# New instruction orders in the first unit and the last stage of a four-layer conditioned residual stack, with the last pair in halves and two pairs' x1 moved to ScalarE

## The reference, cut to what matters

```python
x = x + einsum('bct,bcd->bdt', x, w0[idx_a]) + bias0[idx_a][:, :, None]       # layer 0, mixes positions
h = silu(lora_linear(x, Wg, Ag, Bg, idx_a)) * lora_linear(x, Wu, Au, Bu, idx_a)
x = x + lora_linear(h, Wd, Ad, Bd, idx_a)                                     # layer 1, hidden size 2048
x = x + x @ W.T + (x @ A[idx_b].T) @ B[idx_b].T * scal[idx_b]                 # layer 2
x = x + einsum('bct,bcd->bdt', x, w3[idx_c])                                  # layer 3, mixes positions
# lora_linear(x, W, A, B, i) = x @ W + (x @ A[i]) @ B[i], rank 16, 8 adapters
```

## Time and profile before

| what | us |
| --- | --- |
| median of 3 runs | 735.73 |
| the runs | 731.42, 735.73, 737.94 |
| the profiled execution's own time | 731.5 |
| its span, first to last instruction | 729.7 |
| mean granted TensorE clock | 0.989 |
| TensorE matmul busy in the span | 697.1 |
| VectorE busy | 558.0 |
| POOL busy | 335.0 |
| ScalarE busy | 261.3 |

### The profile page before, as it was taken

The page is one execution under the profiler, slowest core; times in us unless marked ns, Lnnn a source line. Parts: engine busy times, 40 slices in busy tenths (PEclk is TensorE's granted clock), DMA queues, the critical chain, the costliest instruction groups (busy, mean ns, idle before and its releaser), DMA issues.

```text
span 729.7 us, 10894 instructions
## 1 busy us (share of the span) xinstructions
PE 697.1 (96%) x3658; PEld 596.3 (82%) x3658; DVE 558.0 (76%) x979; ACT 261.3 (36%) x470; POOL 335.0 (46%) x606
## 2 busy tenths in 40 slices
PE   8698999999999999999789999999999999989997
PEld 8576788888888888888668888888888888878996
DVE  8956968797978788789877878786969695865553
ACT  3433423232424232443333242332323231436554
POOL 5863544353435343438174544545353343235531
PEclk9899999999999999999999999999999999999999
DMA  8494843333333342504653232323432234213332
GB/s 245 116 173 134 248 135 102 115 102 116 104 120 109 118 124 85 102 22 159 218 130 106 80 106 84 104 84 100 133 103 84 61 92 162 69 51 102 121 116 94
DMA packets 91752, 84.39 MB, mean 116 GB/s; under 512 B 44721, under 2 KB 73393, under 8 KB 91697
## 3 DMA queue, kind: packets, MB, share of 16 engines
q1 hardware_dynamic: 79984, 52.73, 24.4%
q0 software_dynamic: 11392, 30.95, 14.5%
q10 hardware_dynamic: 320, 0.02, 0.0%
HBM read 70.57 MB, written 13.11 MB: 115 GB/s over the span
## 4 chain that ended last, share of the span: by engine, by line
PE 84%; DVE 10%; issue 4%; ACT 2%; POOL 0%; DVEq 0%; ACTq 0%
PE bank L1685 40%; PE bank L1810 21%; PE bank L1693 6%; PE bank L1820 4%; PE bank L1947 3%; PE bank L1953 3%; DVE XC L1158 2%; PE bank L1985 1%; PE bank L1926 1%; PE bank L1631 1%; PE bank L1655 1%; PE bank L1619 1%; DVE XA L1303 1%; DVE hid L1286 1%; DVE hs L1292 1%
## 5 line engine op out<-in xcount | busy, mean ns | idle before, releaser
L1685 PE MATMUL bank<-XC,WC 128*128 128x512 f32 x1344 | 336.1, 396 | 11.3 <-DVE XC L1158 5.2
L1685 PEld LDWEIGHTS bank<-XC,WC 128*128 128x128 f32 x1344 | 245.9, 190 | 60.1 <-issue 10.3
L1810 PE MATMUL bank<-hs,wds 128*128 128x512 f32 x768 | 185.9, 391 | 0.1
L1810 PEld LDWEIGHTS bank<-hs,wds 128*128 128x128 f32 x768 | 141.8, 188 | 28.5 <-DVE wds L1245 0.5
L545 POOL DMA_INDIRECT BL<-bgtab,poffs x96 | 99.4, 1035 | 132.3 <-PE bank L1693 90.0
L545 POOL DMA_INDIRECT BL<-butab,poffs x96 | 96.4, 1004 | 85.9 <-PE bank L1693 63.5
L815 ACT ACTIVATE hs<-hid 128x512 fp32r<-128x512 f32 x64 | 40.1, 630 | 173.4 <-DVE hid L1286 99.2
L1303 DVE TENSOR_TENSOR XA<-bank,XA 128x512 f32<-128x512 f32 x128 | 87.1, 685 | 19.0 <-PE bank L1810 13.1
L809 ACT ACTIVATE hid<-hid 128x512 f32<-128x512 f32 x48 | 30.3, 633 | 152.4 <-DVE hid L1269 79.7
L587 POOL COPY adsel<-ad_raw 128x32 f32 x256 | 43.5, 219 | 69.0 <-DVE ads L1250 64.7
L1693 PEld LDWEIGHTS bank<-UT,BL 128*128 128x128 f32 x384 | 61.7, 191 | 12.6 <-issue 4.4
(11 more groups left out here) (207 smaller groups left out, 855.8 us busy)
## 6 DMA issues: line engine op xcount, KB each, us to landing
RW<-in_L_cond_Wg_dram SPq DMA_DIRECT2D x16, 512.0 KB
RW<-in_L_cond_Wu_dram SPq DMA_DIRECT2D x16, 512.0 KB
RD<-in_L_cond_Wd_dram SPq DMA_DIRECT2D x16, 512.0 KB, 3.4
out_dram<-XB SPq DMA_DIRECT2D x16, 256.0 KB, 2.0
XB<-in_x_dram SPq DMA_DIRECT2D x8, 256.0 KB, 6.0
x1park<-XB SPq DMA_DIRECT2D x8, 256.0 KB
x2park<-XA SPq DMA_DIRECT2D x8, 256.0 KB
XA<-x1park SPq DMA_DIRECT2D x4, 512.0 KB, 7.1
```

Source lines behind the costliest of these rows:

```text
L1685: last = nc.tensor.matmul(psum[:, :], WC[:, t, left, a, k, :], XC[:, right, b, k, :], start=(first and k == 0 and n == 0), stop=(k == 1 an ...
L1810: last = nc.tensor.matmul(psD[j % 2][:, :], by_feature(wds[:, f, a, :])[:, j % KT, :], hs[:, f, b, j // KT * 512:(j // KT + 1) * 512], sta ...
```

## The change

- **Who makes x1.** `SUMMED = 6`: VectorE adds the biases for pairs 0 to 5 only; pairs 6 and 7 get them from TensorE's bias matmul and are copied by ScalarE. `s_xr` becomes two semaphores (one for each writer), asked through `x1_there`.
- **Start, TensorE.** 12 warming matmuls of 512 columns in place of 24 of 128, and none after the biases; pairs 8 and 9 go behind the first product P1, 10 and 11 behind P6, 14 and 15 ahead of the selects.
- **Start, VectorE and ScalarE.** New lists. T2 (and what it needs) comes ahead of B21, T3, B22, the B table and T1. The zeros of `w0second` and `w3bd` are written by ScalarE. `move_matrices` and `pass_rows` are earlier.
- **Start, POOL and SP.** `select_a` is split in two pairs of quads around pairs 12 and 13; `select_ad(0)` goes behind `gather_b(1, 1)`. The loads of A go ahead of B's and of four x pairs; the eight loads of the down adapters go behind `load_d(0)` and `load_b(1)`, both of which wait until TensorE has done pair 15.
- **Units 0 and 8.** The first silu is ahead of `raw_high`/`sums_high` (unit 0) or between them (unit 8). In unit 0 the sums u3 and half22 come ahead of U's weights on VectorE.
- **Last stage.** Down adapters' splits first on ScalarE, `ud_low(0)` ahead of `hs_low`, `lora_down(3)` behind `layer2(0)`, `ud_high(1)`/`ud_low(1)` earlier, `w3_low` later; pair 15 is done in two halves of 256 columns, and y of pair 14 is copied by VectorE.

```diff
-        XO = [[B11, B21, B22, T3, T2, T1, T4], [B11, B21, T3, T2, B22, T1, T4]]
+        XO = [[B11, T2, B21, T3, T1, B22, T4], [B11, B21, T3, T2, B22, T1, T4]]
...
+        SUMMED = 6
+        def x1_there(pairs):
+            return (s_xr[0], pairs) if pairs <= SUMMED else (s_xr[1], pairs - SUMMED)
...  (SP)
+                load_xin(HP)
+                load_xin(HP + 1)
+                load_a(0)
                 load_b(0)
-                for p in range(HP, HP + XIN):
+                for p in range(HP + 2, PAIRS - 2):
                     load_xin(p)
-                load_a(0)
                 store_b(0)
-                for p in range(HP + XIN, PAIRS):
+                for p in range(PAIRS - 2, PAIRS):
                     load_xin(p)
                 load_idx(2, idx_c)
                 load_u(0)
                 load_g(1)
-                sp.wait_ge(s_xr, HP)
+                load_d(0)
+                load_b(1)
+                sp.wait_ge(s_xr[0], SUMMED)
                 for n in range(ADAPTERS):
                     sp.dma_start(ad_raw[:, :, n * RANK:(n + 1) * RANK],
                                  ad[n].rearrange("(k p) r -> p k r", p=P)).then_inc(s_ald, 16)
-                load_d(0)
                 load_u(1)
-                load_b(1)
...  (POOL)
+                select_a(0, 0, cols)
+                select_a(0, 1, cols)
                 late += adapters(24, 8)
                 for p in range(HP + 4, PAIRS):
                     if p == PAIRS - 2:
-                        for q in range(HQ):
-                            select_a(0, q, cols)
+                        select_a(0, 2, cols)
+                        select_a(0, 3, cols)
...
-                    select_ad(unit, cols)
+                    if unit:
+                        select_ad(unit, cols)
                     gather_b(b + 1, 1)
+                    if unit == 0:
+                        select_ad(unit, cols)
...  (ScalarE)
+                def u_window_start(unit, n):
+                    if unit == 0:
+                        silu(unit, n, 0, 0)
+                    act.wait_ge(s_sel, SHOTS * (unit // UNITS + 1))
                     raw_high(U, unit, None if unit == 0 else 2 * (unit - 1) + 1, s_uld)
+                    if unit:
+                        silu(unit, n, 0, 0)
                     sums_high(U, unit)
...  (VectorE, start)
+                move_matrices()
+                xr_sum(0)
+                xr_sum(1)
+                pass_rows()
+                xr_sum(2)
                 g_combine(0)
                 xr_sum(3)
+                xr_sum(4)
                 raw_low(G, 0)
-                xr_sum(4)
-                pass_rows()
                 xr_sum(5)
                 xc_low(0, B11)
-                xr_sum(6)
-                xr_sum(7)
                 t3_sum(0)
+                t2_sum(0)
+                sums_low(G, 0)
+                xc_low(0, T2)
                 xc_low(0, B21)
-                b_low(0)
-                t2_sum(0)
-                xc_low(0, B22)
-                xc_low(0, T3)
-                sums_low(G, 0)
-                t1_sum(0)
-                xc_low(0, T2)
                 a_low(0, 0)
                 a_low(0, 1)
+                xc_low(0, T3)
+                t1_sum(0)
+                b_low(0)
                 a_sum(0)
-                t4_sum(0)
                 xc_low(0, T1)
+                xc_low(0, B22)
                 a_low(0, 2)
                 a_low(0, 3)
-                move_matrices()
+                t4_sum(0)
+                u_low(0, 0)
+                sum_u2(0)
+                u_low(0, 1)
                 xc_low(0, T4)
-                u_low(0, 0)
                 p_combine(0)
-                u_low(0, 1)
...  (TensorE)
-                        nc.tensor.matmul(psE[:, 0:P], ones[:, :], ones[:, :], start=True, stop=True)
+                        nc.tensor.matmul(psE[:, :], ones[:, :], hs[:, 0, 0, 0:512], start=True, stop=True)
...
                     p1_product(0, G)
-                    layer0(HP + 2)
-                    layer0(HP + 3)
+                    layer0(HP)
+                    layer0(HP + 1)
...
                     p6_product(0, G)
+                    layer0(HP + 2)
+                    layer0(HP + 3)
                     adapters_in(0, 0)
                     layer0(HP + 4)
                     layer0(HP + 5)
...
                     p5_product(0, G)
                     adapters_in(0, 1)
+                    layer0(HP + 6)
+                    layer0(HP + 7)
                     select(0, 0)
                     select(0, 1)
-                    layer0(HP + 6)
-                    layer0(HP + 7)
...
-                warm(24)
+                warm(12)
                 biases_to_all()
-                warm(4)
...  (last stage)
                 lora_down(2)
-                lora_down(3)
                 for p in range(PAIRS):
                     layer2(p)
+                    if p == 0:
+                        lora_down(3)
...
-                layer3(PAIRS - 1)
+                for c in range(2):
+                    last_layer3(c)
```

More of the change, by code:

```diff
@@ L481, in store @@
                     d, q = p // 2, p % 2
-                    sp.wait_ge(c_y, p + 1)
-                    sp.dma_start(out_pairs[p * P:(p + 1) * P, :], y[d % 2][q]).then_inc(c_out[d % 2][q], 16)
+                    parts = 2 if p == PAIRS - 1 else 1
+                    for c in range(parts):
+                        at = slice(c * FEAT // parts, (c + 1) * FEAT // parts)
+                        sp.wait_ge(c_y, p + 1 + c)
+                        sp.dma_start(out_pairs[p * P:(p + 1) * P, at], y[d % 2][q][:, at]).then_inc(c_out[d % 2][q], 16)
                 for d in range(DUOS // 2):
@@ L824, in gate_window @@
                         hs_high(unit - 1, 0, 1, 4)
-                    p_high(unit)
                     if i:
+                        p_high(unit)
                         ad_high(unit - 1)
-                    silu(unit, n, 0, 0)
+                        silu(unit, n, 0, 0)
+                    else:
+                        u_window_start(unit, n)
                     silu(unit, n, 3, 1)
@@ L970, in y_out @@
                     nc.scalar.activation(y[d % 2][q], psR[q][:, :], ACT.Copy).then_inc(c_y, 1)
+                bd_high(0)
+                bd_high(1)
                 ud_high(0)
[L973 to L977 removed]
+                hs_high(ALL - 1, 0, 1, 4)
+                for n in range(TABS):
                     table_high(n)
@@ L995, in _ @@
                         bd_high(p // 2 + 3)
-                    if p == 1:
-                        ud_high(1)
-                x3_high(PAIRS - 1)
-                y_out(PAIRS - 1)
+                for c in range(2):
+                    last_x3_high(c)
+                for c in range(2):
+                    last_y_out(c)
             @block.vector
@@ L1092, in w3_identity @@
                                             ident2.unsqueeze(1).to_broadcast([P, HP, POS]), ALU.add).then_inc(s_w3i, 1)
-                def layer3_zeros():
-                    for s in range(2):
-                        nc.vector.memset(w3bd[s][:, :, :].bitcast(f32), 0.0).then_inc(s_zero, 1)
                 def move_matrices():
@@ L1359, in gate_window @@
                         ad_low(unit - 1)
-                    if unit not in (1, UNITS):
+                    if unit not in (0, 1, UNITS):
                         sum_u3(n)
@@ L1604, in _ @@
                         xt_low(p // 2 + 1)
+                    if p == 2:
+                        ud_low(1)
                     if p and p + 1 < PAIRS:
                         w3_low(p + 1)
-                    if p == 2:
-                        ud_low(1)
-                x3_low(PAIRS - 1)
+                p = PAIRS - 2
+                dve.wait_ge(c_l3, p + 1)
+                dve.wait_ge(c_out[p // 2 % 2][p % 2], 16 * (p // 4))
+                nc.vector.tensor_copy(y[p // 2 % 2][p % 2], psR[p % 2][:, :]).then_inc(c_y, 1)
+                p = PAIRS - 1
+                for c in range(2):
+                    dve.wait_ge(c_x3h, PAIRS + c)
+                    high, low = (halves(x3s[p % 2][:, a, :])[:, c, :] for a in range(2))
+                    nc.vector.tensor_tensor(low, x3_of(p)[:, c, :], high.bitcast(f32), ALU.subtract).then_inc(c_x3l, 1)
             @block.tensor
@@ L1985, in layer3, with last_layer3 @@
                         last = nc.tensor.matmul(psR[q][:, :], w3bd[q][:, a, :], x3s[p % 2][:, b, :], start=(n == 0), stop=(n == 2))
+                    last.then_inc(c_l3, 1)
+                def last_layer3(c):
+                    p = PAIRS - 1
+                    pe.wait_ge(c_x3l, PAIRS + c)
+                    if c == 0:
+                        pe.wait_ge(c_w3l, PAIRS)
+                        pe.wait_ge(s_x2, 2 * DUOS)
+                        pe.wait_ge(c_y, p - 1)
+                    at = slice(c * QT, (c + 1) * QT)
+                    for n, (a, b) in enumerate(THREE):
```

(2 more changed lines are left out.)

127 lines of the change are left out of this document (74 added, 53 removed).

## The result

| | kernel before | changed kernel |
|---|---|---|
| median of four runs, us | 733.97 (731.42 to 737.94) | 722.45 (719.96 to 726.11) |
| ratio to before, 95% interval | | 0.9845 (0.9811 to 0.9879) |
| profiled execution: time, span, us | 731.5, 729.7 | 726.11, 724.3 |
| mean granted clock of TensorE in it | 0.989 | 0.991 |

The changed kernel is 1.5% faster: 11.5 us by the medians, where 12.7 were forecast. The two profiled executions are only 5.4 us apart, because the one of the changed kernel is the slowest of its four.

The account below looks back on a forecast made before the run. TensorE's products fill 96% of the span, so reordering only wins back its gaps and low-clock stretches: 7.0 (start) + 0.6 (unit 8) + 4.8 (last stage) = 12.4 us, from the 735.73 median to 723, range 715 to 731.

Parts of the forecast that it names:

- the 12.4 of the sum: Whole kernel: 7.0 us for the start, 0.6 for unit 8 and 4.8 for the last stage.
- T2 and the first clock: Start: T2's low part at 25.4 us, so the 5.17 us gap and the clock's fall behind it are gone.
- The rival on the clock: First unit: two short idles drop TensorE to 1.2 GHz throughout, 10 us slower, 746; chance 0.07.
- POOL's copies: Start: quads 0 and 1 end at 28.3 us; the last eight go fast beside idle VectorE, end at 35.3.
- POOL is held by VectorE: Start: VectorE busy while quads 2 and 3 are copied; P5 and all behind 5.6 us later, 729; chance 0.15.
- Unit 1: Late adapters delay B's gathers: TensorE stalls until 79.8 us, next product near 80.1, a gain of 7.6 there.
- the late down adapters cost more: Start into unit 1: the down adapters' loads are four us later, 4 us less gain, 727; chance 0.20.
- the loads don't bind: Unit 1: the rows land before 76.5 us, 3 us better, 720; chance 0.11.
- The step that failed: From about 95 to 620 us TensorE has hardly a gap and unchanged code; gains must come from elsewhere.
- Unit 8: Unit 8: silu no longer behind the high sums, TensorE's 1.31 us wait goes; 0.6 us won, bounds 0 and 1.3.
- The last stage: Last stage: 2.6 us up to ranks2_turned(0), 1.0 from waits for u2, 1.2 at the end; 4.8 in all.
- The sign named for it: End of the kernel: under 1.5 us from the last lora_out to the last copy's start.

Follow-up runs that it names:

- late silus: Changed kernel with ScalarE's first silu of units 0 and 8 back behind U's high parts and sums: 715.64 us, ratio 0.9801; again on another chip 715.07 us.
- T2 late: Changed kernel with only the order of the start's splits on ScalarE and VectorE undone, T2's behind B21, B, B22, T3 and T1 sum: 719.25 us, ratio 0.9845.
- the start alone: Changed kernel with the edits of the last stage undone, all edits ahead of the last unit kept: 730.26 us, ratio 0.9933.
- in the experiment: Changed kernel with four unused sums of 512 columns on VectorE just ahead of a_sum, while POOL copies: 717.31 us in one run.
- third chip: Chip of the third group of runs; the unaltered changed kernel, run again there, took 714.28 us, ratio 0.9788 to the kernel before.
- bd splits later: Changed kernel with the splits of bd on ScalarE behind the last hs and first table piece, as before the change: 724.58 us, ratio 0.9873.
- first chip: Chip of the first group of runs; the unaltered changed kernel, run again there, took 725.15 us, ratio 0.9871 to the kernel before.

## Why the prediction was right, point by point

**The time.** 723 was forecast and 722.45 measured. That it is so close is in part luck: on the three chips of the experiments the same kernel won 8.8 us (first) and 15.7 us (third) by the medians, on both sides of the 12.4 of the sum.

**T2 and the first clock.** T2's low part ended at 25.6 us (25.4 forecast), the gap of 5.17 us ahead of P6 shrank to 1.11, the clock stayed at 2.4 GHz. Right. The idle of about a microsecond that is left does not lower the clock as a rule, but it can: TensorE was at 1.2 GHz for 3.4 us from 26.0 us on behind 1.11 us of idle (VectorE busy), for 10.2 and 20.5 us from 17 on behind 1.2 us (late silus, T2 late), for 3.4 us from 53.9 on behind 1.38 us (the start alone). The rival on the clock had the right mechanism and too large a price: no run shows a loss of 10 us to it, and 10.2 us at 1.2 GHz cost 1.4 at P1 of the U window. One reading was short: behind the 2.54 us of idle the kernel before ran at 1.2 GHz for 3.4 us, not 2, since the stretch read ended at 64.

**POOL's copies.** Quads 0 and 1 ended at 27.7 (28.3 forecast), the last eight ran alone in 2.20 us and ended at 34.4 (35.3). P5 started at 36.48 (37.3), `adapters_in(0, 1)` at 39.20 (40.0), P1 of the U window at 56.95 (57.0). Each step held within a microsecond, and the rival "POOL is held by VectorE" fell, because VectorE did run out; its mechanism is real, but its price of 1.05 us for each copy is a mean of short and long ones. A copy takes as long as the instruction beside it: 0.75 us beside sums of 512 columns in the experiment, 1.28 beside the long instructions of VectorE (752 and 1282 ns in the earlier trace rows).

**Unit 1.** Here the number was right for the wrong reason. Forecast was a stall until 79.8 us and the next product near 80.1; the third chip shows the stall until 79.33 and the product at 79.78. But the steps in between were not those:

- The down adapters were through the queue at 59.6 us, not 63.4, because the eight loads took 12.98 us to issue and not 16.43.
- POOL's first copy of `select_ad(0)` came at 63.2, not at 66, and its gathers began at 67.0, not at 69.8.
- They landed 4.4 us after the last issue (third chip), not 2, because the eight stores of x1 ran beside them (1.8 without). I had taken 2 us from a store of 256 KB on a quiet queue and had not looked at what SP issues in that stretch.

Two errors of 2 to 3 us cancelled. The rival "the late down adapters cost more" fell with the first of them, and "the loads don't bind" fell too: the stores bound instead.

**The pauses.** What the profile after lacks of the forecast (5.4 us won, not 12.4) is at two places, and neither is a step of the change. In units 0 and 1 the 9.7 us won at P1 fall to 4.4; in unit 9 another 3.5 go. The step that failed is the sentence that from about 95 to 620 us there is nothing to win or lose: the kernel before has a pause of 2.08 us there itself, with 3.4 us at the lower clock behind it, together 3.5 us. The third chip's profile, without any, is 16.2 us shorter than that of the kernel before; less these 3.5 it is 12.7, close to the 12.4 of the sum.

**Unit 8.** 0.6 was forecast, 0.4 measured: the U window's start gained 0.4 in the profile after, and the late silus cost 0.4 between the downs of units 7 and 8 (59.0 against 58.6 us).

**The last stage.** 4.8 forecast, 4.4 measured. `ranks2_turned(0)` starts 23.1 us behind the last unit's first down product, where it was 25.0: 1.9 in place of 2.6; with the bd splits later it is 21.5, which is 3.6. `lora_down(0)`, which was to start 0.8 us earlier, starts 9.3 us behind that product where it was 8.3, so 1.1 later; with the bd splits later it is 7.7. There is the miss: moving the bd splits ahead of `ud_high` on ScalarE was costed as a gain for `lora_down(0)`, and the subtraction that POOL then makes was not followed to what VectorE does at that moment. The wait for x2 is covered, as forecast, and no wait for u2 above 0.2 us follows. The end of the kernel before starts with this row of TensorE, not shown so far, the last `lora_out`:

```profile
723.47 0.41 PE L1972 MATMUL bank<-XC,WC 96*128 96x256 f32 x2
```

From it to the end of the span it was 6.2 us (729.7), and now it is 5.1 (719.23 to 724.3): 1.1 to 1.2 us, as forecast. The sign named for it failed all the same: ScalarE's last two copies start 1.9 and 2.3 us behind it, not under 1.5.

**The bounds.** The start's bounds of 3 and 10 us held: 4.4 in the profile after, 8.0 on the third chip. The total was to lie between 715 and 731 us; the four executions of the result do (720.0 to 726.1). The changed kernel's single executions on the chips of the experiments go from 713.8 to 728.6, and the third chip's median of 714.28 lies just below.

## What to carry to other kernels

Follow a moved operation to the end of its chain, the other engines' work at that moment included: the two losses that this change brought with it (bd's subtraction beside `w2_identity`, the stores of x1 beside the gathers) each came from an instruction that was on no one's critical path. A gather's or load's time to land is a property of what else is in flight, so take it from the stretch where it will run. And compare the two profiles stage by stage before a stage's gain is called lost: executions of one kernel on one chip differed by up to 10.5 us (724.3 to 734.8, the start alone), and part of such differences lies at places that no change touches, as in unit 9.

## What the runs showed of the hardware that I had not expected

- **Pauses of TensorE with late signals.** In units 1 and 9, 2 to 4 us long, followed by 3.4 or 6.8 us at 1.2 GHz. On the first chip all four profiles have the one in unit 9 (3.90, 3.89, 3.86 and, with bd later, 1.97 us), and two of them, the changed kernel and its first half, also the one in unit 1. The first profiles of both kernels look like that chip's. None of the eight profiles on the other two chips has the one in unit 9. What causes them is open: no wait, no transfer and no other engine that the profile shows accounts for them. But all six profiles with a pause also lack records: their packed traces hold 6213 to 6393 semaphore events, the other eight 8565 to 8569, and they have the landing of 41 to 74 of some 395 transfers, the others of 328 to 394. So a transfer that accounts for the pauses could be missing there, and whether the lost records and the pauses have one cause, the recording itself among them, is not shown. The DMA queues are half idle in unit 9 (a share of 0.39 from 370 to 382 us), and the same instructions ran with and without. The kernel before lost 4 us to the first chip against the third (733.99 to 729.96), the changed one 11 (725.15 to 714.28). Whether its order is more exposed, or a pause only shows where there is no other wait to hide it, was not tried.
- **The two engines take the port from each other in both directions, for a whole instruction.** VectorE's additions of 0.28 us took 1.36 and 1.41 us beside POOL's subtractions of 1.30 and 1.33; POOL's copies of 0.30 us took 0.75 beside VectorE's sums of 0.77. A mean over several hides it.
- **Stores on SP's queue delay POOL's gathers.** With 2 MB of stores beside them the rows landed 2.6 to 4.4 us after the last issue (six profiles), without them 1.7 (two). The DMA share from 60 to 77 us was 1.04 with them and 0.66 without (third chip).
